# First attention of a two-layer kernel: scores from three products on half the contraction rows, instead of two on stacked copies

## What is computed

```python
x = x + _L0_xattn_ref(_layernorm(x), ctx, ctx, mask, Wq, Wk, Wv, Wo)
# 16 heads of 64: Qh = (queries @ Wq).reshape(n, t, 16, 64), Kh and Vh likewise from ctx
energy = jnp.einsum('nqhd,nkhd->nhqk', Qh, Kh) * scale
energy = jnp.where(mask == 0, -1e+20, energy)
attention = jax.nn.softmax(energy, axis=-1)
heads_out = jnp.einsum('nhqk,nkhd->nqhd', attention, Vh)
return heads_out.reshape(n, t, 16 * 64) @ Wo
```

## Time and profile before

| | us |
|---|---|
| median of 3 runs | 1425.09 (1423.35 to 1429.33) |
| span of the profiled execution, first to last instruction | 1427.3 |
| PE busy | 1138.1 (80% of the span) |
| PE weight loads busy | 860.6 (60%) |
| DVE busy | 798.9 (56%) |
| ACT busy | 627.2 (44%) |
| POOL busy | 507.8 (36%) |

### The profile page before, as it was taken

The page is one execution under the profiler, slowest core; times in us unless marked ns, Lnnn a source line. Parts: engine busy times, 40 slices in busy tenths (PEclk is TensorE's granted clock), DMA queues, the critical chain, the costliest instruction groups (busy, mean ns, idle before and its releaser), DMA issues. The chain is left out here.

```text
span 1427.3 us, 30050 instructions
## 1 busy us (share of the span) xinstructions
PE 1138.1 (80%) x10895; PEld 860.6 (60%) x10896; DVE 798.9 (56%) x2325; ACT 627.2 (44%) x1171; POOL 507.8 (36%) x491
## 2 busy tenths in 40 slices
PE   2499999999999998338899455488999654988896
PEld 1166777777777776335788323355666343777775
DVE  7177887787688775758101163466777522444443
ACT  4177786787687774200222032144555312332231
POOL 2656454455544241300444230789300022011112
PEclk9899999999999999655899769799999856999999
DMA  6122223213212120700265415455311231111010
GB/s 235 52 60 63 66 57 78 55 46 79 65 46 67 47 50 20 238 28 2 96 185 170 110 42 186 124 161 158 91 47 39 73 95 62 19 27 28 19 15 8
DMA packets 80218, 110.88 MB, mean 78 GB/s; under 512 B 11552, under 2 KB 58400, under 8 KB 79712
## 3 DMA queue, kind: packets, MB, share of 16 engines
q1 hardware_dynamic: 69632, 88.23, 21.2%
q0 software_dynamic: 10464, 21.01, 6.4%
HBM read 59.86 MB, written 24.70 MB: 59 GB/s over the span
## 5 line engine op out<-in xcount | busy, mean ns | idle before, releaser
L542 DVE CUSTOM_DVE_ANT_0 masked<-sc,mask_bias 128x512 f32<-128x512 f32 x256 | 175.5, 686 | 58.0 <-issue 41.1
L518 DVE TENSOR_TENSOR e_t_lo<-et,e_t_hi 128x512 f16<-128x512 f32 x256 | 176.7, 690 | 50.9 <-ACT e_t_hi L484 48.5
L491 ACT ACTIVATE e<-masked,neg_max 128x512 f32<-128x512 f32 x256 | 184.1, 719 | 27.2 <-DVE neg_max L542 26.6
L484 ACT ACTIVATE e_t_hi<-et 128x512 f16<-128x512 f32 x256 | 152.0, 594 | 88.6 <-PE et L435 88.1
L435 PEld LDWEIGHTS et<-ident,e 128*128 128x128 f32 x1024 | 125.6, 141 | 54.1 <-ACT e L491 6.8
L435 PE MATMUL et<-ident,e 128*128 128x128 f32 x1024 | 154.1, 273 | 1.4 <-ACT e L491 0.7
L1266 ACT ACTIVATE d_e<-d_st 128x384 f32<-128x384 f32 (+1 forms) x192 | 98.0, 528 | 117.1 <-PE d_st L1351 101.1
L197 PE MATMUL h_hb<-h_xt_hi,experts_hi 128*128 128x256 f16 x352 | 101.5, 288 | 26.5 <-DVE h_xt_lo L1720 26.5
L197 PE MATMUL ob<-v_hi,e_t_hi 128*128 128x65 f16 x1024 | 119.0, 193 | 0.6 <-DVE e_t_lo L518 0.6
L198 PE MATMUL ob<-v_lo,e_t_hi 128*128 128x65 f16 x1024 | 119.2, 193 | 0.0
L199 PE MATMUL ob<-v_hi,e_t_lo 128*128 128x65 f16 x1024 | 118.4, 193 | 0.0
(11 more groups left out here) (315 smaller groups left out, 2906.6 us busy)
## 6 DMA issues: line engine op xcount, KB each, us to landing
kk<-nat_k SPq DMA_DIRECT2D x128, 128.0 KB, 2.3
raw<-in_fc SPq DMA_DIRECT2D x16, 1024.0 KB
qq<-nat_q SPq DMA_DIRECT2D x128, 64.0 KB, 2.0
mask_raw<-in_mask SPq DMA_DIRECT2D x16, 256.0 KB, 2.8
scratch_stack<-c_qk_hi SPq DMA_DIRECT2D x32, 128.0 KB
scratch_stack<-c_qk_lo SPq DMA_DIRECT2D x32, 128.0 KB
d_expert_raw<-in_gate_w POOLq DMA_DIRECT2D x8, 512.0 KB, 4.4
d_expert_raw<-in_up_w POOLq DMA_DIRECT2D x8, 512.0 KB, 4.0
```

What stands on the lines that cost most here:

```text
L484: nc.scalar.activation(e_t[u % NBUF].hi[:], et[u % 2][:], ACT.Copy).then_inc(turned_hi, 1)
L491: nc.scalar.activation(e[u % NBUF][:], masked[u % NBUF][:], ACT.Exp, bias=neg_max[:, g % 2, j:j + 1], scale=-1.0).then_inc(exp_ok, 1)
L518: nc.vector.tensor_tensor(e_t[u % NBUF].lo[:], et[u % 2][:], e_t[u % NBUF].hi[:], ALU.subtract).then_inc(turned_lo, 1)
L542: nc.vector.tensor_tensor_reduce(masked[u % NBUF][:], sc[j % 2][:], mask_bias[g // PAIRS % 2][:, j % QT, :], -SCALE0, 3e38, ALU.add, ALU.m ...
```

## The change

The stacked copies are gone, with their DMAs, tiles and semaphores. `split` writes hi and lo of q and k straight into double-buffered tiles `heads`, rows 0 to 63 for head 0 of the pair and 64 to 127 for head 1. A unit's scores are three products on the 64 rows of its head. The heads alternate: unit j is head j % 2 and tile j // 2, and two units are scored together, every second step, with their six matmuls in turn on the upper and the lower rows. The wait on masking is for both banks. SP only loads masks. normalize(., 0) moves from step 1 to step 4, as head 0's last value product now comes later.

```diff
-                def stack(g):
-                    i = g % 2
-                    sp.wait_ge(split_done, COPY0["k", g] + 1)
...
-                load_mask(0)
-                load_mask(1)
-                stack(0)
-                load_mask(2)
-                load_mask(3)
-                for g in range(PAIRS0 - 1):
-                    stack(g + 1)
-                    if g // PAIRS + 1 < B and g % PAIRS < QT:
-                        load_mask((g // PAIRS + 1) * QT + g % PAIRS)
+                for n in range(NT):
+                    load_mask(n)
...
-                        if at >= 1:
-                            pool.wait_ge(stacked[0], STACKED * at)
-                            pool.wait_ge(stacked[1], STACKED * at)
-                        hi, lo = nat[kind][:, 0, :], nat[kind][:, 1, :]
+                        if at >= 2:
+                            pool.wait_ge(scores, (at - 1) * UNITS)
+                        hi, lo = heads[kind][at % 2].hi[:], heads[kind][at % 2].lo[:]
...
-                def score(u):
-                    g, j = u // UNITS, u % UNITS
-                    a, qt = j // QT, j % QT
-                    if j % QT == 0:
-                        pe.wait_ge(stacked[a], STACKED * (g + 1))
+                def score_both(u):
+                    g, qt = u // UNITS, u % UNITS // 2
+                    if u % UNITS == 0:
+                        pe.wait_ge(split_done, COPY0["q", g] + 1)
                     if u >= 2:
-                        pe.wait_ge(masked_ok, u - 1)
-                    stat = qq[g % 2][:, a, qt * P:(qt + 1) * P]
-                    pe.matmul(sc[j % 2][:], stat, kk[g % 2][:, a, 0, :], start=True, stop=False)
-                    pe.matmul(sc[j % 2][:], stat, kk[g % 2][:, a, 1, :], start=False, stop=True).then_inc(scores, 1)
+                        pe.wait_ge(masked_ok, u)
+                    q, k = heads["q"][g % 2], heads["k"][g % 2]
+                    for n, (stat, mov) in enumerate(((q.hi, k.hi), (q.hi, k.lo), (q.lo, k.hi))):
+                        for a in range(2):
+                            rows = slice(a * DK, (a + 1) * DK)
+                            mm = pe.matmul(sc[a][:], stat[rows, qt * P:(qt + 1) * P], mov[rows, :], start=(n == 0), stop=(n == 2))
+                            if n == 2:
+                                mm.then_inc(scores, 1)
...
-                    if u < units:
-                        score(u)
+                    if u < units and u % 2 == 0:
+                        score_both(u)
...
-                    dve.wait_ge(pv_done, g * UNITS + (a + 1) * QT)
+                    dve.wait_ge(pv_done, (g + 1) * UNITS - 1 + a)
...
-                        if u % UNITS == 1 and u >= UNITS:
+                        if u % UNITS == 4 and u >= UNITS:
                             normalize(u // UNITS - 1, 0)
```

More of the change, by code:

```diff
@@ L242, in phase_attention0 @@
         raw = [sb(f"raw{i}", [P, 512]) for i in range(NRAW)]
-        nat = {"q": sb("nat_q", [P, 2, S], F16), "k": sb("nat_k", [P, 2, S], F16)}
-        qq = [sb(f"qq{i}", [P, 2, S], F16) for i in range(2)]
-        kk = [sb(f"kk{i}", [P, 2, 2, S], F16) for i in range(2)]
+        heads = {kind: [Split(sb, f"{kind}_heads{i}", [P, S]) for i in range(2)] for kind in ("q", "k")}
         o = [sb(f"o{i}", [P, QT, P]) for i in range(2)]
@@ L261, in phase_attention0 @@
         pj_full, copied, added, split_hi, split_done, v_const = (sem(n) for n in ("pj_full", "copied", "added", "split_hi", "split_done", "v_const"))
-        stacked = [sem(f"stacked{a}") for a in range(2)]
         scores, masked_ok, exp_ok = sem("scores"), sem("masked_ok"), sem("exp_ok")
@@ L266, in phase_attention0 @@
         mask_in, bias_ok = [sem(f"mask_in{i}") for i in range(2)], sem("bias_ok")
-        STACKED = 4 * 16
         def v_part(part, n):
@@ L439, in attend @@
                     g, j = u // UNITS, u % UNITS
-                    b, a, head = g // PAIRS, j // QT, (g % PAIRS) * 2 + j // QT
-                    if j % QT == 0 and g >= 1:
+                    b, a, qt, head = g // PAIRS, j % 2, j // 2, (g % PAIRS) * 2 + j % 2
+                    if qt == 0 and g >= 1:
                         pe.wait_ge(normed, 2 * g - 1 + a)
@@ L447, in attend @@
                         vv = (v[b % 2].hi[:, kt, head, 0:DK + 1], v[b % 2].lo[:, kt, head, 0:DK + 1])
-                        mm = three_products(pe, ob[a][:, j % QT, 0:DK + 1], (e_t[u % NBUF].hi[:, kt, :], e_t[u % NBUF].lo[:, kt, :]), vv, kt == 0, kt == QT - 1)
+                        mm = three_products(pe, ob[a][:, qt, 0:DK + 1], (e_t[u % NBUF].hi[:, kt, :], e_t[u % NBUF].lo[:, kt, :]), vv, kt == 0, kt == QT - 1)
                     mm.then_inc(pv_done, 1)
@@ L540, in maximum @@
                     nc.vector.memset(gate[:, u % (2 * UNITS):u % (2 * UNITS) + 1], 0.0)
-                    nc.vector.tensor_tensor_reduce(masked[u % NBUF][:], sc[j % 2][:], mask_bias[g // PAIRS % 2][:, j % QT, :],
+                    nc.vector.tensor_tensor_reduce(masked[u % NBUF][:], sc[j % 2][:], mask_bias[g // PAIRS % 2][:, j // 2, :],
                                                    -SCALE0, 3e38, ALU.add, ALU.min, neg_max[:, g % 2, j:j + 1]).then_inc(masked_ok, 1)
```

## The result

The changed kernel takes 1482.3 us in the median of four runs (1479.4 to 1485.3), the kernel before 1424.2. The ratio is 1.041, 95% interval 1.038 to 1.044: 4% slower, 58 us, where 68 were forecast.

A forecast was written before the change was run, and what follows sets the result against it. PE's own work was taken to bound the first attention. Against the profiled span, 1427.3 + 80.2 - 6.3 - 6.3 = 1494.9 us; from the median, 1425.1 + 67.6 = 1493 us; range 1440 to 1565, about 0.8.

The forecast's parts named there:

- the rival of 1575 us: Score blocks: the two halves of the array do not overlap, 0.64 us more in every pair, 82 us; chance 0.15.
- Weight loads: Score blocks: a load for one half waits for the matmul on that half, 32 us, 1525 us; chance 0.06.
- the rival of the falling clock: First attention: the clock falls in the new stalls of PE, over 1800 us; chance 0.03.
- The faster rival: First attention: the wait costs nothing because DVE is through before PE, 1411 us; chance 0.07.
- the loop: First attention, from a block's scores through both maskings to the next scores: 80.2 us more, matmul time saved included.
- the handover from DVE to PE: From DVE's end to PE's next matmul: 0.24 us at most, taken as 0.23.
- a switch: Change of the array's division into and out of each score block: 0.10 us each, bounds 0 and 0.17.
- pair (6,7): Units 6 and 7 of a group: 3.54 us for 2.90, 0.64 more; 0.98 more where w is added to x.
- pair (4,5): Units 4 and 5 of a group, normalize(0) now before the second masking: with v 4.19 us for 3.75, 0.44 more.
- start: Start of the kernel: all masks queued first, so PE's stall shrinks, 6.3 us less (bounds 4 and 8).
- stacking DMAs: SP's queue in the first attention: PE's waits for these DMAs, 6.3 us in all, gone.
- Two expected signs: Profile after: PE idle about 1.2 us before score blocks in three pairs a group; PE's busy share from 10 tenths to 8.

The follow-up runs named there:

- the first experiment: The kernel before, with its 128-row products, but two units scored together every second step and the wait for both banks: 1485.4 us, ratio 1.042.

## Why the prediction was right

Direction and mechanism held, point by point. PE's own work was the bound, and a wait put into its order moved the time though every engine had room on average. The halves do run side by side (three rounds, 0.22 apart), the rival of 1575 us was wrong, and when the two heads were forced onto the same rows, the stage took 68.6 us more, where this rival was put at 82. Weight loads did not show: rounds are 0.22 apart, with the loads of the next round starting along with the matmuls of this one. The granted clock stayed at 1.00 from 63.2 us to the end of the stage, through stalls of up to 1.1 us, so the rival of the falling clock was wrong. The faster rival was wrong at the point named for it: the second masking ended 3.38 us after the block began, far beyond PE's own work of 2.4.

The sum came out 10 us high, and the terms tell why:
- the loop: forecast 80, measured 69. The term that was mis-sized is the handover from DVE to PE: 0.06 in pairs (2,3) and (4,5) (322.70 to 322.76) and not 0.23, which was read from a matmul of another stage. Against that the first transposes behind a switch take 0.66 and not 0.60. Net 0.10 less in pair (2,3) and 0.2 in (4,5).
- in pair (6,7) the handover takes 0.16 (330.13 to 330.29; this block starts at 326.75). With the second masking ending 0.07 later than forecast, that brings 3.53 for 3.54:

```profile
329.44 0.69 DVE L519 CUSTOM_DVE_ANT_0 masked<-sc,mask_bias 128x512 f32<-128x512 f32 x1
...
330.29 0.39 PE L403 MATMUL sc<-k_heads_hi,q_heads_hi 64*128 64x512 f16 x2 [0.22 <-DVE neg_max L519]
```

  The difference goes with the waits in the code. The scores of a new group wait for the split of q as well as for the masking; those of pairs (4,5) and (6,7) for the masking alone. In the first experiment the scores at steps 0 and 4 of a group have a second wait, for the stacking, and take 0.16, and those at step 6, with one wait, 0.07. The matmul of the earlier trace rows stands behind two waits too. No run changed the number of waits by itself.
- a switch: forecast 0.10 in and 0.10 out, from the column strips of the earlier trace rows, measured 0.10 and 0.10, plus the 0.06 in the transposes that the rows did not hold. Pair (0,1) was forecast 0.01 shorter and is 0.04 longer for it.
- pair (4,5), with normalize(.,0) in its loop: forecast 0.44 more with v, measured 0.24, by the same handover; the experiment that moved it back by a step shows the term by itself, 8 to 10 us.
- start: forecast 6.3, measured 7.1; stacking DMAs: forecast 6.3, and the waits for them are gone.

Two expected signs were off in size. PE idles 0.84 in the plain pairs and not 1.2: a matmul is listed 0.165 longer than the spacing to the next, which covers that much of the idle time, and the handover was shorter. And PE's busy share was to fall to 8 tenths; it is 9 (17.94 and 18.79 of 20). The number of stalls, 65 on neg_max, is just below the 70 to 90 named.

What stays open is whether a second wait alone costs the 0.1, and why the last batch's groups are slower when the old products are scored in pairs with both banks read first.

## What to carry over

When an engine is the bound, read which earlier result each of its waits asks for and how many units lie between; shortening that distance from two units to one turned an engine with room (DVE, 79% busy) into the one that held the path, and putting both maskings first in its order gave back two thirds of the loss. Saved columns have to be set against what a change of the array's shape costs in every block: here 0.21 us saved and about 0.25 paid. And the only gain of a change can be a queue that it empties as a side effect; it is worth trying alone.

## What the runs showed of the hardware

- Matmuls on rows 0 to 63 and on rows 64 to 127 overlap fully: three rounds of two 512-column float16 products start 0.22 us apart, as full-height ones do one by one, with results in two PSUM banks. On the same 64 rows the rounds take 0.44.
- TensorE starts them together even when the program has three matmuls on one half ahead of the first on the other half: same block length (2.53 and 2.54 us) in both orders, the second 0.010 us behind the first and not 0.003. The Trainium skill (TensorE: Matmul & The Clock Gate, The mechanism) says that matmuls start strictly in program order; these rows disagree with that.
- Changing between full height and half height costs 0.10 us at each change here, and the four transposes behind a change back take 0.66 us and not 0.60.
- From the end of the maximum's instruction on DVE to the start of the matmul that waits for it takes 0.06 us where the matmul has that wait alone, and 0.15 where the code has a second wait in front of it, already met (pairs (2,3) and (6,7) of the changed kernel, 30 groups each, within 0.002). In the first experiment pair (2,3) has the second wait, and takes 0.15 too.
